# Cross attention's softmax without the second taking of its scores: weights turned on PE, divided on GpSimd, in a decoder kernel of two layers

## The reference

```python
q = (x @ Wq).reshape(B, N, 16, 64)
k = (context @ Wk).reshape(B, 77, 16, 64)
v = (context @ Wv).reshape(B, 77, 16, 64)
sim = einsum('bihd,bjhd->bhij', q, k) * 64 ** -0.5
attn = softmax(sim, axis=-1)
out = einsum('bhij,bjhd->bihd', attn, v)
return out.reshape(B, N, 1024) @ Wo
```

## Time and profile before

| what | value |
|---|---|
| times of 3 runs | 845.19, 846.94, 856.15 us (median 846.94) |
| profiled execution: time, span | 846.87 us, 845.1 us |
| granted TensorE clock, mean | 0.938 |
| PE, PEld busy | 718.3 us (85%), 538.8 us (64%) |
| DVE, ACT, POOL busy | 518.2 us (61%), 417.1 us (49%), 205.9 us (24%) |
| DMA queues | 72.30 MB, mean 86 GB/s |
| landing of the relative scores' load (median) | 5.5 us |

### The profile page before, as it was taken

The page is one execution under the profiler, slowest core; times in us unless marked ns, Lnnn a source line. Parts: engine busy times, 40 slices in busy tenths (PEclk is TensorE's granted clock), DMA queues, the critical chain, the costliest instruction groups (busy, mean ns, idle before and its releaser), DMA issues. The chain is left out here.

```text
span 845.1 us, 22574 instructions
## 1 busy us (share of the span) xinstructions
PE 718.3 (85%) x9462; PEld 538.8 (64%) x9462; DVE 518.2 (61%) x1447; ACT 417.1 (49%) x1188; POOL 205.9 (24%) x212
## 2 busy tenths in 40 slices
PE   5788998999998798999874887898888888988873
PEld 3466776677776576776664685666666666766641
DVE  1343665555557655655565575777878877788732
ACT  3745656456556355566432122345555554555531
POOL 5210011111101110115314022334333334333200
PEclk9989999999999799999998796999999999999975
DMA  9534444233444214444422110000000000110000
GB/s 361 206 123 129 153 154 154 104 126 93 141 154 154 107 48 154 153 151 153 144 90 101 50 41 17 8 11 15 14 12 11 12 11 13 15 16 11 5 5 6
DMA packets 48261, 72.30 MB, mean 86 GB/s; under 512 B 2832, under 2 KB 43280, under 8 KB 45472
## 3 DMA queue, kind: packets, MB, share of 16 engines
q1 hardware_dynamic: 45120, 61.80, 21.5%
q0 software_dynamic: 2320, 5.18, 2.8%
q10 hardware_dynamic: 720, 3.88, 1.2%
HBM read 32.38 MB, written 38.47 MB: 84 GB/s over the span
## 5 line engine op out<-in xcount | busy, mean ns | idle before, releaser
L403 POOL TENSOR_TENSOR rext<-rext,ones 128x1008 f32<-128x1008 f32 x16 | 29.9, 1867 | 320.5 <-ACT rext L919 320.5
L934 ACT ACTIVATE sc<-sc,nmxa 128x128 f32<-128x128 f32 x256 | 78.2, 388 | 7.0 <-DVE nmxa L1149 6.3
L972 ACT ACTIVATE pTb<-bank 77x512 f32<-77x512 f32 x128 | 66.8, 590 | 7.3 <-PE bank L486 7.3
L1199 DVE TENSOR_REDUCE nmb<-bank 128x4 f32<-128x308 f32 x128 | 53.7, 472 | 16.6 <-PE bank L486 16.5
L1438 DVE TENSOR_TENSOR k<-bank,k_sb 128x512 f32<-128x512 f32 x64 | 41.2, 685 | 35.5 <-PE bank L486 35.5
L1145 DVE TENSOR_TENSOR sc<-bank,rel 128x512 f32<-128x512 f32 x64 | 41.1, 684 | 21.3 <-PE bank L486 21.3
L464 POOL TENSOR_SCALAR k<-k 128x256 f32<-128x256 f32 x16 | 13.8, 860 | 160.2 <-ACT k L1048 160.2
L486 PE MATMUL bank<-k,xdT 128*128 128x512 f32 x96 | 49.3, 654 | 0.0
L919 ACT ACTIVATE rext<-bank 128x512 f32<-128x512 f32 x64 | 35.6, 592 | 27.0 <-PE bank L486 27.0
L534 PE MATMUL bank<-k_sb,sc 128*128 128x128 f32 x256 | 42.3, 289 | 7.0 <-ACT sc L934 4.7
L486 PE MATMUL bank<-nmT,k_sb 32*77 32x128 f32 x1024 | 47.6, 280 | 0.0
(11 more groups left out here) (267 smaller groups left out, 1744.5 us busy)
## 6 DMA issues: line engine op xcount, KB each, us to landing
rel_dram<-rext SPq DMA_DIRECT2D x16, 2040.0 KB
rel<-rel_dram SPq DMA_DIRECT2D x16, 960.0 KB, 5.5
...
wb<-w_b ACTq DMA_DIRECT2D x1, 1604.0 KB, 16.5
...
```

The lines of the kernel that those rows point to most:

```text
L403: G.tensor_tensor(rext[:, :, 0:MAX_REL - 1], rext[:, :, MAX_REL - 1:MAX_REL].broadcast_to(shape), ones[:, 0:1].unsqueeze(2).broadcast_to(s ...
L934: last = A.activation(sc[:, h, :], sc[:, h, :], ACT.Exp, bias=nmxa[:, h:h + 1])
L972: A.activation(dst[0:C, 4 * i:4 * i + 4, :], bank[b][0:C, :].rearrange("p (a i) -> p a i", a=4), ACT.Exp).then_inc(exped["b"], 1)
L1199: V.tensor_reduce(nmb[:, 32 * i:32 * i + 4], bank[b][:, 0:4 * C].rearrange("p (a j) -> p a j", a=4), AX.X, ALU.max, negate=True).then_inc( ...
```

## The change

- Cross attention's scores are taken once. DVE finds the maxima (`b_max`) and adds their negatives while it writes the scores to a new SBUF tile `pB` (`b_less`), which frees the banks. ACT takes the exponentials in place (`b_exp`), DVE the sums and reciprocals, POOL multiplies the weights by them in place (`b_n0`, `b_n1`), PE turns the 16 heads' 128x77 weights (`b_t0` to `b_t3`, into banks 6, 7, 4, 5), and ACT and DVE copy two banks each to `pTb`. `b_u0` and `b_u1` become plain copies.
- The second taking, the turn of the maxima, their injection, the sums by ones and their reciprocals go.
- Values, output and projections of self-attention, the relative scores, cross attention's values and the context's values wait for the maxima or subtractions that free their banks of the next scores, and are placed behind these. The relative scores of slice i+1 stand at the start of round i, the self turns of slice i-1 behind them.
- The pipeline is deeper: self turns and values of slice i-1, cross scores of slice i-2, turns, values and output of slice i-3, logits of slice i-4, ranks and slots of slice i-6 share a round.
- POOL sends one slice per round from round 12 on, rather than a batch at once.
- `pB` shares its memory with the keys' weights `wk` and the tile `rb`; `x1` has three buffers. Some semaphores of the second layer are shared with the first layer's.

The core of the diff:

```diff
 ORDER1 = {
-    "pe": ("b_inj:-1 a_t2 a_t3 a_qkv:2 a_v b_sm0:-1 b_sm1:-1 b_v0:-1 b_v1:-1 rel_last:2 a_out b_out:-1 rel:2 "
-            "v0 b_r:-1 b_x b_lg:-1 r_rank:-2 a_s:1 b_q b_s0 b_s1 a_t0:1 b_st0 b_nm a_t1:1 b_st1").split(),
-    "dve": ("a_t3 r_b:-2 a_qkv:2 a_div b_u0:-1 rel_last:2 b_u1:-1 a_add a_st a_ag b_add:-1 b_st:-1 b_ag:-1 "
-            "b_norm:-1 a_ln v0 b_lg:-1 r_a:-1 r_c:-2 a_m0:1 b_qhi b_m0 b_m1 b_m2 b_m3 a_m1:1 a_t1:1").split(),
-    "act": ("a_e1 b_nm:-1 a_t0 a_e2 a_e3 a_t2 b_e0:-1 b_e1:-1 b_e2:-1 b_e3:-1 a_qkv:2 a_v b_rc:-1 a_ln rel0:2 "
-            "rel1:2 b_ln:-1 rel2:2 v0 rel3:2 b_r:-1 b_x b_qlo r_a:-1 a_e0:1").split(),
-    "pool": "r_send:-16 rel_fill:2".split(),
-    "sp": "load_rel:1 store_rel:2".split(),
+    "pe": ("rel:1 r_rank:-6 b_x:-2 a_t0:-1 a_t1:-1 b_t0:-3 a_t2:-1 a_t3:-1 b_t1:-3 b_t2:-3 b_t3:-3 a_s b_q:-2 "
+            "b_s0:-2 b_s1:-2 a_v:-1 a_qkv:2 b_v0:-3 b_v1:-3 a_out:-1 b_out:-3 rel_last:2 b_r:-4 v0:-2 b_lg:-4").split(),
+    "dve": ("b_ag:-4 r_a:-5 v0:-3 r_b:-5 r_c:-6 a_t1:-1 a_t3:-1 b_t1:-3 b_t3:-3 a_m0 b_qhi:-2 a_m1 b_m0:-2 "
+            "b_m1:-2 b_l0:-2 b_m2:-2 b_l1:-2 b_l2:-2 a_div:-1 b_norm:-4 b_u0:-3 b_m3:-2 b_u1:-3 a_qkv:2 b_l3:-2 "
+            "b_sum0:-2 a_add:-1 b_add:-3 rel_last:2 a_st:-1 b_rec0:-2 a_ag:-1 b_st:-3 b_sum1:-2 a_ln:-1 "
+            "b_rec1:-2 b_lg:-4").split(),
+    "act": ("b_t2:-3 b_ln:-4 b_qlo:-2 a_e0 a_e1 a_v:-1 a_qkv:2 b_e0:-2 b_e1:-2 a_e2 a_e3 b_e2:-2 b_e3:-2 b_r:-4 "
+            "a_ln:-1 v0:-2 rel0:2 r_a:-4 rel1:2 b_x:-1 rel2:2 rel3:2 a_t0 a_t2 b_t0:-2").split(),
+    "pool": "rel_fill:2 b_n0:-1 b_n1:-1 r_send:-12".split(),
+    "sp": "store_rel:2 load_rel:2".split(),
 }
...
+        early = sb("early", [P, H * C])
+        wk = early[:, 0:WK_N]
+        pB = early[:, :].rearrange("p (h j) -> p h j", j=C)
         wb = sb("wb", [P, WB_N])
...
+        rb = early[:, 0:XC * P].rearrange("p (c i) -> p c i", c=XC)
         v0 = sb("v0", [P, H, XH])
         nmxa = sb("nmxa", [P, H])
+        nmxb, sumb, recb = sb("nmxb", [P, H]), sb("sumb", [P, H]), sb("recb", [P, H])
...
+            def b_even_(j):
+
+                def f(t):
+                    pool.wait_ge(recips["b"], 2 * t + 1 + j)
+                    part = slice(8 * j, 8 * j + 8)
+                    G.tensor_tensor(pB[:, part, :], pB[:, part, :], recb[:, part].unsqueeze(2).broadcast_to([P, 8, C]),
+                                    ALU.mult).then_inc(b_even, 1)
+                return f
+
             def send(t):
-                if t not in BATCH_AT:
-                    return
-                lo, hi = BATCH_AT[t]
-                pool.wait_ge(r_slots, 2 * sum(1 for b in BATCHES if b[1] <= hi) - 1)
-                if lo == 0:
+                pool.wait_ge(r_slots, 2 * sum(1 for b in BATCHES if b[0] <= t) - 1)
+                if t == 0:
                     pool.wait_ge(st_zero, 32)
-                for s in range(lo, hi):
-                    for k in range(2):
-                        G.indirect_dma_start(
-                            out=xg_dram, out_offset=bass.IndirectOffsetOnAxis(
-                                ap=to_slot[:, 2 * s + k:2 * s + k + 1], axis=0),
-                            in_=x_all[:, s, :], in_offset=None).then_inc(st_xg, 16)
-
-            run(ORDER1["pool"], {"rel_fill": rel_fill, "r_send": send}, BEGUN1)
+                for k in range(2):
+                    G.indirect_dma_start(
+                        out=xg_dram, out_offset=bass.IndirectOffsetOnAxis(
+                            ap=to_slot[:, 2 * t + k:2 * t + k + 1], axis=0),
+                        in_=x_all[:, t, :], in_offset=None).then_inc(st_xg, 16)
+
+            run(ORDER1["pool"], {"rel_fill": rel_fill, "b_n0": b_even_(0), "b_n1": b_even_(1), "r_send": send}, BEGUN1)
...
             def a_qkv_(t):
                 pe.wait_ge(ld_xT[t % 4], 16 * (t // 4 + 1))
-                need(pe, a_pT_act, 2 * (t - 1))
-                need(pe, r_mid, 4 * t)
+                need(pe, maxed["a"], 4 * (t - 2) + 3)
                 mm(bank[2][:, 0:P], w("a0_wq"), xT_ld[t % 4][:])
...
                 pe.wait_ge(a_kv, t + 1)
                 pe.wait_ge(r_lastc, t + 1)
-                need(pe, var["a"], t - 1)
-                need(pe, oT_ready["a"], t - 1)
-                need(pe, r_mid, 4 * t)
+                need(pe, maxed["a"], 4 * (t - 1))
+                need(pe, oT_ready["a"], t - 2)
+                need(pe, var["a"], t - 2)
...
             def a_scores(t):
                 pe.wait_ge(a_kv, t + 1)
-                need(pe, var["a"], t)
+                need(pe, a_pT_act, 2 * t)
...
             def a_turn(i):
                 def f(t):
                     pe.wait_ge(exped["a"], 4 * t + i + 1)
+                    if t + 2 < B:
+                        pe.wait_ge(r_mid, 4 * (t + 2) + i + 1)
+                    need(pe, oT_ready["a"], t)
+                    need(pe, var["a"], t)
...
             def a_values(t):
+                if t + 1 < B:
+                    pe.wait_ge(maxed["a"], 4 * (t + 1) + 1)
                 pe.wait_ge(a_pT_act, 2 * t + 2)
                 pe.wait_ge(a_pT_dve, 2 * t + 2)
...
             def a_out(t):
                 if t == 0:
                     pe.wait_ge(ld_wb, 16)
+                if t + 1 < B:
+                    pe.wait_ge(maxed["a"], 4 * (t + 1) + 2)
                 pe.wait_ge(oT_ready["a"], t + 1)
...
             def b_x(t):
                 pe.wait_ge(normed["a"], t + 1)
-                pe.wait_ge(v_lo, t + 1)
-                pe.transpose(bank[6][:, 0:P], x1[t % 2][:], ident).then_inc(xT_ps["a"], 1)
+                need(pe, v_lo, t)
...
             def b_q_(t):
                 pe.wait_ge(xT_ready["a"], t + 1)
-                pe.wait_ge(v_hi, t + 1)
-                need(pe, lg_sb, t)
+                need(pe, b_pT_act, 2 * t)
+                need(pe, b_pT_dve, 2 * t)
...
                 def f(t):
                     pe.wait_ge(b_qhi if j else b_qlo, t + 1)
                     if j == 0:
-                        need(pe, var["b"], t)
+                        need(pe, b_pT_act, 2 * t - 1)
...
-            def b_nm(t):
-                pe.wait_ge(maxed["b"], 4 * t + 4)
-                pe.transpose(bank[5][:, 3 * P:4 * P], nmb[:], ident).then_inc(nm_ps, 1)
-
-            def b_turn(j):
-                def f(t):
-                    pe.wait_ge(maxed["b"], 4 * t + 2 + 2 * j)
-                    if j:
-                        pe.wait_ge(nm_sb, t + 1)
-                    for c in range(4 * j, 4 * j + 4):
-                        for i in range(2):
-                            mm(bank[(4 if j else 6) + i][0:C, (c % 4) * P:(c % 4 + 1) * P], k0[half(i), t, c, :],
-                               q0[half(i), c, :], start=(c % 4 == 0), stop=False)
+            def b_turn(i):
+
+                def f(t):
+                    pe.wait_ge(b_even, 2 * t + 1 + i // 2)
+                    if i == 0:
+                        pe.wait_ge(v_lo, t + 1)
+                        if t + 1 < B:
+                            pe.wait_ge(xT_ready["a"], t + 2)
+                    if i == 1:
+                        need(pe, var["b"], t)
+                    if i == 2:
+                        pe.wait_ge(v_hi, t + 1)
+                    if i == 3:
+                        need(pe, lg_sb, t - 1)
+                        if t - 3 in BATCH_AT:
+                            pe.wait_ge(r_slots, 2 * sum(1 for b in BATCHES if b[1] <= t - 2) - 1)
+                    for a in range(4):
+                        last = pe.transpose(bank[(6, 7, 4, 5)[i]][0:C, a * P:(a + 1) * P], pB[:, 4 * i + a, :], ident)
+                    last.then_inc(turned, 1)
                 return f
 
...
-            def b_sums_(j):
-
-                def f(t):
-                    pe.wait_ge(exped["b"], 4 * t + 2 + 2 * j)
-                    for u in (2 * j, 2 * j + 1):
-                        for s in range(4):
...
             def b_values(j):
 
                 def f(t):
-                    pe.wait_ge(exped["b"], 4 * t + 2 + 2 * j)
+                    pe.wait_ge(b_pT_act, 2 * t + 1 + j)
+                    pe.wait_ge(b_pT_dve, 2 * t + 1 + j)
+                    if t + 1 < B:
+                        pe.wait_ge(maxed["b"], 4 * (t + 1) + 1 + 2 * j)
                     for u in range(2):
...
+                    pe.wait_ge(maxed["b"], 4 * t + 1 + 2 * i)
                     need(pe, oT_ready["b"], 2 * (t - 1) + 1 + i)
                     mm(bank[4 if i else 6][0:C, :], cT[:, t, :], w("c0_wv", i * 512, (i + 1) * 512)).then_inc(v_ps, 1)
...
             def b_r(t):
                 pe.wait_ge(normed["b"], t + 1)
+                if t + 2 < B:
+                    pe.wait_ge(maxed["b"], 4 * (t + 3))
+                else:
+                    pe.wait_ge(b_pT_dve, 2 * B)
+                need(pe, lg_sb, t)
+                need(pe, r_slots, 2 * sum(1 for b in BATCHES if b[1] <= t - 1) - 1)
                 pe.transpose(bank[5][:, 0:P], x_all[:, t, :], ident).then_inc(xT_ps["b"], 1)
 
...
```

(69 more changed lines are left out.)

79 lines of the change are left out of this document (33 added, 46 removed).

## The result

The changed kernel takes **809.16 us** (median of 4, 808.87 to 810.73) beside 847.16 for the kernel before on the same chip (median of 4): ratio 0.9535, interval 0.947 to 0.960. I had forecast 826. The sign was right, and so was the main mechanism (PE's list gets shorter); the gain was nearly twice what I summed: 38 us, not 21. The profiled execution took 808.87 us with a span of 807.0.

The account below looks back on a forecast made before the run. PE was taken to bound the 16-slice loop: rounds of 21.4 us put the last `b_out` at 421, a 32.5 us tail made 453.5 against 474.95, 21 us less, so 826 us; range 809 to 852.

Parts of the forecast that it names:

- the price of a round: Steady loop round: 23.86 less 1.1 idle less 1.9 of PE work, plus 0.5 for slips, 21.4 us.
- the new turns: PE's list per round: 16 added transposes of 128x77 at 0.145 each, 2.3 us, bounds 1.9 to 2.8.
- the waits: PE per round: the 1.1 us of idle goes, 0.5 us is added for slips behind DVE.
- Removed: PE's list per round: second cross scores, maxima's turning and injection (3.32), sums by ones (0.87) go, 4.19 us.
- irregular rounds: Loop time beyond steady rounds, from PE's issue stops, lower clock after them and batch routing: 20 us, 22 before.
- about 19 us: DVE's busy time per round, rising from 13.9, nearly full with 2 us to spare instead of 10.
- The hand-drawn margins: DVE's release points per round against PE's needs, everything in time by a hair; six within 0.2 us.
- Rival B: DVE's in-order queue becomes the bound: rounds 22.6 to 23.8 us, kernel 847, range 839 to 857; chance 0.24.
- Filling: Loop's start: first scores at 34.06, rounds 0 to 2 of 9, 14.5 and 18 us, round 3 at 76.
- The tail: Last `b_out` to turning of tokens: first send 7.7 us after, 16 queued sends; 32.5 us, 12.9 longer.
- Rival C: Better than forecast: no slips, rounds of 20.9 us, issue stops shrink with fewer instructions; kernel 813 us, chance 0.15.
- Rival D: PE's clock falls inside the block of 32 transposes: 3.0 us a round more, kernel 874 us; chance 0.08.

## Why the prediction was right or wrong

**The failed step is the price of a round,** "21.4 us a round", bounds 20.9 and 23. Measured: 20.06, below even the floor. Over 13 full rounds that alone is 17 us. Two of its terms were mis-sized: the new turns, 2.3 for a measured 1.84, and the waits, a net 0.6 less for a measured 1.5 less. The other errors nearly cancel. This table is by PE's starts, in us from the span's start or of length (rounded, so its column adds up to 15.3):

| step | forecast | measured | off |
|---|---|---|---|
| round 3 starts | 76 | 81.0 | +5.0 |
| rounds 3 to 15 with irregular | 298 | 278.6 | -19.4 |
| round 16 | 18.3 | 16.9 | -1.4 |
| round 17 | 15 | 14.1 | -0.9 |
| round 18 to the last `b_out` | 13.5 | 14.8 | +1.3 |
| tail to the turn | 32.5 | 32.6 | +0.1 |
| turn of the tokens | 453.5 | 438.0 | -15.5 |

What failed inside the round, 23.86 to 20.06, from starts of both timelines:
- *Removed*, 4.19: the items hold 4.15. This term was right. The 1.38 of the run with scores taken twice does not speak to it, being for narrower products.
- *New turns*, 2.3: 1.84, so 0.46 a round too much. I took the row of four self turns at 0.145. From start to start it holds four turns of 0.11 and 0.14 more at its end, before a product of 64 rows. In the new order four turns with others behind them take 0.44; only the last twelve have a product of fewer rows behind them and hold 0.08 more (12 in 1.40, 24 in 2.72 with turns taken twice). The row was not late: its four exponentials were done at 317.64, a microsecond ahead of it.
- *Waits*, "1.1 us idle removed, 0.5 for slips added", together -0.6: measured -1.5. Idle marked on PE fell only from 1.13 to 0.70; the other 1.1 stood in longer rows. The self turns fell from 2.59 to 1.82, the router and normed-row items with the last column from 1.79 to 1.34 (these hold marked waits of 0.34 and 0.26 before), `v0` from 2.09 to 1.72; `b_out` and the projections got 0.17 shorter and `a_v` and `b_v` 0.23 longer. 0.9 a round.

The self turns' part can be read from the weight loads of the kernel before, PE's second timeline, with ScalarE's first four exponentials ahead of them:

```profile
316.36 1.28 ACT L934 ACTIVATE sc<-sc,nmxa 128x128 f32<-128x128 f32 x4 [0.28 <-DVE nmxa L1149]
```

```profile
318.62 0.42 PEld L534 LDWEIGHTS bank<-k_sb,sc 128*128 128x128 f32 x4
319.20 0.87 PEld L486 LDWEIGHTS bank<-q,k 64*77 64x77 f32 x16 [0.17 <-DVE nmb L1199]
...
323.10 0.42 PEld L534 LDWEIGHTS bank<-k_sb,sc 128*128 128x128 f32 x4 [0.16 <-issue]
323.90 0.42 PEld L534 LDWEIGHTS bank<-k_sb,sc 128*128 128x128 f32 x4 [0.39 <-ACT sc L934]
```

Half of the 0.77 is a wait of 0.39 for the last exponentials, which PE's own row of eight turns (1.46) does not mark. The rest lies at the ends of the groups, where the next weights are loaded 0.16 to 0.23 late each time that products of another number of rows begin; one such place is left in the new block. Why it is so, and what made the other items longer, no run isolates.

Together 0.46 + 0.9 is the 1.3 by which the round was off. The Trainium skill, "TensorE: Matmul & The Clock Gate", Part 4, has about 275 ns for a bf16 transpose inside a kernel. This case's fp32 rows have 110 at clock 1.00, in three kernels.

**Fewer full rounds.** Rounds 14 and 15 are 19.9 and 18.25; round 15 has no relative scores left to take. I had charged both in full: 2 of the 19.4. The 20 for irregular rounds came out at 19.8, but by luck. Of the 22 of before, 9.4 lay in the two rounds with the first batch's routing (28.0 and 29.1 long), the rest in stops and what followed them. Now rounds 12 and 13 (29.4 and 25.0) hold 14.2, and the rounds with stops only 5.6.

**DVE.** "about 19 us": 17.37 busy. I added durations, while neighbours overlap by 0.08 (155.72 to 156.49 is 0.77 for two rows of 0.47). The hand-drawn margins were right to 0.1: `b_v0` 0.2 ahead of its need (measured 0.2), `b_v1`'s bank 0.1 behind it (measured 0.1). **Rival B was four short DVE instructions a round away:** with all maxima twice the kernel takes 846.84, B's 847, and from the first of them on the round grows. B fell because the one release that comes late costs 0.1 a round as the kernel stands, not because DVE has time in plenty.

**POOL.** 1.4 a multiply: 1.21. Covered, as said. The rule that two-SBUF products stretch while POOL works came true in the first batch's pick; this is DVE's timeline after.

```profile
270.96 1.80 DVE L1330 TENSOR_TENSOR one_hot<-k_sb,r_c 128x64 f32<-128x64 f32 x1
272.80 1.82 DVE L1332 SCALAR_TENSOR_TENSOR r_ok<-one_hot,lg 128x64 f32<-128x64 f32 x1
```

Two products of some 0.2 took 1.8, 3.2 too much against my 3.8, while the adds out of PSUM kept 0.684 in the mean over the kernel. POOL's fills of that round stand beside them, from 270.82 to 274.54. That agrees with the Trainium skill, "GPSIMD Engine Reference", § Key points. The whole pick, 9.1 us from 269.20 to 278.31 with these 3.2 in it, stood ahead of the copies of the self weights. What it led to is on PE's timeline: a wait, and then half clock, 2.09 where the round has 1.14 for the same self scores.

```profile
279.88 2.09 PE L496 MATMUL bank<-kbd,qa 32*128 32x512 f32 x8 [6.93 <-DVE pTa L1190]
```

**Filling.** 5 us too low. Rounds 0 and 2 were nearly right, 9.7 for 9 and 18.8 for 18; round 1 took 18.4 for 14.5 (43.83 to 62.21). On PE's timeline its sixteen turns behind an idle PE take 3.50 (46.70), at half pace, and waits of 0.98 and 1.99 follow, at 51.18 and 54.31.

**The tail** was right in each part. These are PE, then POOL, around it; they answer to the earlier trace rows.

```profile
398.45 3.64 PE L496 MATMUL bank<-pTb,v 77*32 77x128 f32 x64 [4.85 <-DVE pTb L1275]
402.02 3.41 PE L496 MATMUL bank<-wb,oTb 128*128 128x128 f32 x16
...
438.00 2.87 PE L739 MATMUL bank<-k_sb,pTa 128*128 128x128 f32 x12 [0.91 <-DMA pTa<-xg_dram]
```

```profile
413.01 0.96 POOL L440 DMA_INDIRECT xg_dram<-x_all,to_slot  x1 [11.22 <-DVE to_slot L1373]
...
431.93 0.96 POOL L440 DMA_INDIRECT xg_dram<-x_all,to_slot  x1 [0.30 <-issue]
```

The pick of six slices holds back the copies (4.85). The first send comes 7.6 after the last `b_out` (7.7 forecast). Then 16 sends go unbroken, 1.26 apart, and the last stands 6.1 before the turn.

**Rival C** (faster rounds, fewer stops) came nearest in its number, 813, in part by luck: its rounds of 20.9 were still 0.8 too long, and it shared the filling that was forecast 5 us too short. Its stops went from five of 1.4 to 1.8 us to three of 0.9 to 1.2, which is 8.3 to 3.1 us. **Rival D** has nothing for it in the full rounds: the 32 turns ran at clock 1.00. By the Trainium skill, "TensorE: Matmul & The Clock Gate", Part 4, transposes don't count as busy for the clock as other products do; the trace doesn't bear this out. Here 32 of them in 3.66 us were followed by no fall; a wait of DVE's making (all four maxima twice) and a block of eight-column products were. In round 1 sixteen turns alone ran at a granted 0.54, and the self scores behind them at full pace (1.14).
